# Gates z and n of a GRU step with the state as stationary operand, in four column groups

## The chip, the cores and the metric

The kernel runs on one core of a Trainium2 chip. The metric is the time of one execution in microseconds, as the device gives it. It is one program, written by hand for each engine: TensorE (PE), VectorE (DVE), ScalarE (ACT), GpSimd (POOL) and SyncE (SP) each have an instruction queue of their own, and semaphores join them.

## The reference

A GRU runs over 256 time steps of 16 sequences with 512 features, and its states go through a mixture of 8 experts of which each token uses the best two. The result is added to the input.

```python
def cell(h, x):
    gi = x @ W_ih + b_ih
    gh = h @ W_hh + b_hh
    i_r, i_z, i_n = jnp.split(gi, 3, axis=-1)
    h_r, h_z, h_n = jnp.split(gh, 3, axis=-1)
    r = jax.nn.sigmoid(i_r + h_r)
    z = jax.nn.sigmoid(i_z + h_z)
    n = jnp.tanh(i_n + r * h_n)
    h_new = (1.0 - z) * n + z * h
    return (h_new, h_new)
...
scores = jnp.einsum('btd,ed->bte', x, Wg)
topk_s, topk_i = jax.lax.top_k(scores, TOP_K)
probs = jax.nn.softmax(topk_s, axis=-1)
...
for e in range(E):
    h = jax.nn.silu(jnp.einsum('btd,hd->bth', x, W1[e])) * jnp.einsum('btd,hd->bth', x, W2[e])
    y = y + w[..., e:e + 1] * jnp.einsum('bth,dh->btd', h, W3[e])
...
x = x + _L0_ffn_ref(_L0_cond_ref(cond_2048, x, ...), ...)
```

All data are fp32. x is 16 x 256 x 512, W_ih and W_hh are 512 x 1536, the experts are 352 wide.

## The kernel before

Every fp32 matrix product is made of f16 products. A value is scaled and split into a high and a low f16 part (`whh[:, 0]` and `whh[:, 1]`, `hlog[..., 0/1, :]`), and three or four of the products of parts are summed in fp32 in PSUM. Features lie on the partitions: K = 4 blocks of P = 128 features, B = 16 columns for the sequences.

The recurrence is serial, T = 256 steps. One step on TensorE is `recur(t)`. The weights are the stationary operand (128 x 128) and the state is the moving one. First come 16 matmuls of the low weights of gate r with the high state (L1351, 16 columns), which wait for the semaphore value H_HI: VectorE's write of the high f16 part of the new state (L1080, first of two). Then, once the low part is there (H_LO, L1082), come 16 matmuls of r's high weights with both parts side by side (L1357, 32 columns). Then come 32 matmuls for n into `gn_ps` and 32 for z into `gz_ps` (L1366): 4 blocks of output, 4 of contraction, high and low weights behind each other, 32 moving columns each. Each of the three products counts `gh_ready` up by one.

PSUM is not cleared between steps. ScalarE seeds it for the next step (`seed`, L796): half the input projection of r or z, or half the bias of n, written to both halves, the matmuls add to it, and VectorE adds the two halves of the state (`halves`, L1054, a reduce over a pair).

The chain of a step on VectorE and ScalarE is `gru_step` and `gru_acts`: rpre (L1054), sigmoid (L810), hn (L1054), rh = r * hn (L1063), npre (L1067), tanh (L817), zpre (L1054), sigmoid of minus z (L819), nmh = n - h (L1073), znh (L1077), the new state as f16 (H_HI) and as fp32 (both L1080), and H_LO (L1082). `GRU` names these VectorE steps, and `gru(t, name)` is the value of the semaphore `gru_ops` at each. `behind_r(t)` and `behind_z(t)` put small work of the projection, the weight scaling and the routing between them.

All other work of TensorE is placed between two `recur` calls by a list, `blocks(t)`: input projections for four steps at a time (`project`, L1388, banks `gi_ps` and `b_ps`), for t from FIRST = 52 on an expert tile every four steps (A and B: the two up products, L1422; T and X: transposes; D0 and D1: the down product, L1458), and the routing of 128 tokens every eight steps (R1 and R2). 51 expert tiles run beside the recurrence and 20 behind it, in the tail. VectorE and ScalarE have their share of this work behind their part of each step; `choose(g)` (L1155 to L1176) is the routing part on VectorE. GpSimd's gathers and scatters, and SyncE's loads, wait for `gh_ready` to reach `behind_n(t)`.

## Time and profile before

| | us |
|---|---|
| time, median of 2 runs | 1504.82 |
| the two runs | 1501.98 and 1507.65 |
| span of the profiled execution, first to last instruction | 1501.1 |
| busy in it: TensorE / VectorE / ScalarE / GpSimd | 1409.4 / 1043.8 / 896.3 / 415.8 |
| chain that ended last | PE 83%, DVE 10%, issue 3% |

The profile is of one execution. It gives a span, and no other time of its own is recorded; the span lies 0.9 us under the lower of the two timed runs and 3.7 under their median. The busy time of an engine is what its instructions cover; on TensorE matmuls overlap, and their ends are modelled, so the distance between starts is the better measure of what one costs.

### The profile page before, as it was taken

How to read it: one execution, taken by the hardware profiler on the slowest of the kernel's cores; microseconds unless marked ns; L12 is line 12 of the kernel's file. 1: busy time of each engine (PE TensorE's matmuls, PEld its weight loads, DVE VectorE, ACT ScalarE, POOL GpSimd, SP SyncE). 2: the span in 40 equal slices, each digit the busy share in tenths (PEclk: the TensorE clock that was granted, in tenths of full speed). 3: DMA queues.
4: the chain of work that ended last, by engine and by line, in shares of the span. 5: the costliest groups of instructions: out<-in, count | busy, mean ns of one | idle time of the engine just before them, and what ended most of it. 6: DMA issues, size and time to landing. Idle time of an engine off the chain costs nothing.

```text
span 1501.1 us, 88729 instructions
## 1 busy us (share of the span) xinstructions
PE 1409.4 (94%) x37804; PEld 1227.2 (82%) x37804; DVE 1043.8 (70%) x4116; ACT 896.3 (60%) x2319; POOL 415.8 (28%) x850
## 2 busy tenths in 40 slices
PE   2888878899999999999999999999999999998997
PEld 1888778888888888888888888888888888885664
DVE  7788887777677677777777767776777776764333
ACT  6677675555565556655556555665556655555664
POOL 1011112123322232222332223222333222326443
PEclk9999887899999999999999999999999999999999
DMA  8445413112221222212222122211222212223431
GB/s 290 124 130 140 134 45 90 40 32 40 46 39 39 46 46 40 39 39 46 40 46 40 39 46 46 41 38 40 46 40 46 40 39 47 39 40 79 60 49 16
DMA packets 99011, 88.64 MB, mean 59 GB/s; under 512 B 41407, under 2 KB 74175, under 8 KB 98624
## 3 DMA queue, kind: packets, MB, share of 16 engines
q0 software_dynamic: 17952, 33.64, 12.9%
q1 hardware_dynamic: 80672, 49.32, 11.5%
q8 instruction: 306, 5.01, 1.5%
q14 instruction: 81, 0.66, 0.2%
HBM read 59.12 MB, written 35.72 MB: 63 GB/s over the span
## 4 chain that ended last, share of the span: by engine, by line
PE 83%; DVE 10%; issue 3%; ACT 1%; POOL 1%; DMA 1%; SPq 0%; DVEq 0%; POOLq 0%; ACTq 0%
PE gn_bank L1366 12%; PE gz_ps L1366 12%; PE y_ps L1458 9%; PE b_ps L1388 9%; PE a_ps L1422 8%; PE b_ps L1422 8%; PE gi_ps L1388 8%; PE gr_ps L1357 6%; PE gr_ps L1351 6%; DVE wexp L1037 2%; PE tr_ps L1436 2%; PE tr_ps L1446 2%; PE tr_ps L1478 1%; DVE npre L1067 1%; DVE nmh L1073 1%
## 5 line engine op out<-in xcount | busy, mean ns | idle before, releaser
L1366 PE MATMUL gz_ps<-hlog,whh 128*128 128x32 f16 x8192 | 246.0, 177 | 6.1 <-issue 6.0
L1366 PE MATMUL gn_bank<-hlog,whh 128*128 128x32 f16 x8192 | 245.2, 177 | 2.4 <-issue 2.2
L625 POOL DMA_INDIRECT out_y<-work,mt x57 | 93.9, 1648 | 546.2 <-PE gz_ps L1366 309.6
L1366 PEld LDWEIGHTS gz_ps<-hlog,whh 128*128 128x128 f16 x8192 | 224.1, 96 | 6.9 <-issue 6.7
L1366 PEld LDWEIGHTS gn_bank<-hlog,whh 128*128 128x128 f16 x8192 | 224.2, 96 | 2.7 <-issue 2.7
L1351 PEld LDWEIGHTS gr_ps<-hlog,whh 128*128 128x128 f16 x4096 | 130.6, 96 | 53.9 <-DVE hlog L1080 32.4
L1351 PE MATMUL gr_ps<-hlog,whh 128*128 128x16 f16 x4096 | 141.9, 170 | 31.3 <-DVE hlog L1080 28.3
L1388 PE MATMUL b_ps<-xs,wih 128*128 128x64 f16 x4752 | 162.3, 197 | 3.4 <-issue 2.1
L1458 PE MATMUL y_ps<-wexp,work 128*128 x639 | 159.0, 382 | 1.9 <-ACT work L845 1.9
L1388 PEld LDWEIGHTS b_ps<-xs,wih 128*128 128x128 f16 x4752 | 153.3, 101 | 5.1 <-issue 3.5
L810 ACT ACTIVATE rs<-rpre,sc 128x64 f32<-128x64 f32 x256 | 88.0, 344 | 112.7 <-DVE rpre L1054 112.5
L1388 PE MATMUL gi_ps<-xs,wih 128*128 128x64 f16 x4464 | 145.5, 194 | 4.7 <-issue 3.4
L1388 PEld LDWEIGHTS gi_ps<-xs,wih 128*128 128x128 f16 x4464 | 137.8, 99 | 6.7 <-issue 6.2
L1357 PE MATMUL gr_ps<-hlog,whh 128*128 128x32 f16 x4096 | 142.3, 177 | 1.0 <-issue 0.9
L636 POOL DMA_INDIRECT meta<-meta_sb,pos_i x64 | 66.0, 1031 | 242.4 <-PE gn_bank L1366 109.8
L1054 DVE TENSOR_REDUCE rpre<-gr_ps 128x64 f32<-128x128 f32 x256 | 73.8, 288 | 76.9 <-PE gr_ps L1357 74.5
L1357 PEld LDWEIGHTS gr_ps<-hlog,whh 128*128 128x128 f16 x4096 | 121.2, 96 | 1.3 <-issue 1.0
L1422 PE MATMUL a_ps<-wexp,xgt 128*128 x732 | 119.9, 313 | 0.2 <-issue 0.2
L1422 PE MATMUL b_ps<-wexp,xgt 128*128 x732 | 119.3, 313 | 0.0
L796 ACT ACTIVATE gn_bank<-bhn,sc 128x128 f32<-128x128 f32 x256 | 93.4, 365 | 40.0 <-DVE hn L1054 33.7
L839 ACT ACTIVATE hid<-work,hscale 128x352 f16<-128x352 f32 x71 | 41.8, 588 | 124.8 <-DVE hscale L1221 124.8
L1054 DVE TENSOR_REDUCE hn<-gn_bank 128x64 f32<-128x128 f32 x256 | 73.5, 287 | 51.3 <-PE gn_bank L1366 46.1
(217 smaller groups left out, 2550.3 us busy)
## 6 DMA issues: line engine op xcount, KB each, us to landing
wexp<-in_w_units SPq DMA_DIRECT2D x46, 256.0 KB, 3.8
x_raw<-in_x_feat SPq DMA_DIRECT2D x32, 256.0 KB, 3.7
out_y<-in_x_tok SPq DMA_DIRECT2D x16, 512.0 KB
h_tok<-xrow SPq DMA_DIRECT2D x32, 256.0 KB, 2.0
wexp<-in_w_hh SPq DMA_DIRECT2D x4, 768.0 KB, 6.8
wexp<-in_w_inproj SPq DMA_DIRECT2D x4, 768.0 KB, 11.8
wexp<-in_w_units SPq DMA_DIRECT2D x15, 192.0 KB, 4.5
mt<-meta SPq DMA_DIRECT2D x71, 1.0 KB, 1.7
```

The source lines that it names most:

```text
L625: pool.indirect_dma_start(out=out, out_offset=bass.IndirectOffsetOnAxis(ap=mt[:, j % RING, 0:1].bitcast(I32), axis=0), in_=ysc[y_slot(j)], ...
L636: pool.indirect_dma_start(out=meta, out_offset=bass.IndirectOffsetOnAxis(ap=pos_i[:, i:i + 1], axis=0), in_=meta_sb[:, g, i], in_offset=No ...
L796: S.activation(gh[:], values.unsqueeze(2).to_broadcast([P, K, 2, B]), ACT.Copy, scale=scale(SC_SEED)).then_inc(seeded, 1)
L810: S.activation(rs[:], rpre[:], ACT.Sigmoid, scale=scale(SC_INV)).then_inc(sig_r, 1)
L839: S.activation(hid16[:, 0, 0:HE], hid[:], ACT.Copy, scale=hscale[:, 0:1]).then_inc(hid_hi, 1)
L1054: op(V.tensor_reduce(dst, gh[:].rearrange("p k a b -> p k b a"), AX_X, ALU.add))
L1351: pe.matmul(gr_ps[:, j, 0], whh[:, 1, k, j * P:(j + 1) * P], h[:, k, 0], start=False, stop=False, skip_group_check=True)
L1357: mm = pe.matmul(gr_ps[:, j], whh[:, 0, k, j * P:(j + 1) * P], h[:, k], start=False, stop=True, skip_group_check=True)
L1366: mm = pe.matmul(dst[:, j], whh[:, i, k, m * P:(m + 1) * P], h[:, k], start=False, stop=True, skip_group_check=True)
L1388: mm = pe.matmul(BATCH_BANKS[bank][:, (m - first) * BTOK:(m - first + 1) * BTOK], wih[:, p, w_part, (b * K + k) * P:(b * K + k + 1) * P], ...
L1422: mm = pe.matmul(dst, xT[x_slot(j)][:, a * K + k], part[:, k], start=(i == 0 and k == 0), stop=(i == 2 and k == K - 1))
L1458: mm = pe.matmul(y_ps[:], hidT[:, PARTS[i][0] * HB + b], parts[PARTS[i][1]][:, b], start=((i, b) == DOWN[0]), stop=((i, b) == DOWN[-1]))
```

## The change

z and n are computed with the operands exchanged. The state of one block, 16 sequences with their high and low parts (32 columns, now laid out as pairs), is the stationary operand, and 256 columns of weights move: the 8 blocks of z and n, 32 features of each. The result of group g lies on the partitions 32g to 32g+31 of one bank, `zn_bank`, one partition for each sequence and part, one column for each feature. There are four groups, for each of the 4 blocks of contraction, high and low weights behind each other: 32 matmuls. The bank isn't seeded; the first matmul of each group clears it. z and n now share one count of `gh_ready`, two a step in place of three.

VectorE transposes n's half and z's half back in 32 x 32 blocks (`turn`) into the first two of three columns of `n_parts` and `z_parts`. The third holds n's bias (written once) and the input projection of z (`place_z`, ScalarE, each step). `total` sums the three. Gate r stays as it was. Some steps now write in place.

```diff
-    GRU = "R HN R_HN N_PRE Z N_H Z_NH H_HI H_NEW H_LO".split()
+    GRU = "R N_TURNED HN R_HN N_PRE Z_TURNED Z N_H Z_NH H_HI H_NEW H_LO".split()
...
-        return 3 * t + 2
+        return 2 * t + 2
...
-        hlog = sb("hlog", [P, 2, K, 2, P], F16)
+        hlog = sb("hlog", [P, 2, K, P, 2], F16)
...
+        n_parts = sb("n_parts", [P, K, B, 3])
+        z_parts = sb("z_parts", [P, K, B, 3])
...
-        gn_bank = ps("gn_bank", [P, 512])
-        gn_ps = gn_bank[:, 0:K * 2 * B].rearrange("p (k a b) -> p k a b", k=K, a=2)
-        gz_ps = ps("gz_ps", [P, K, 2, B])
+        zn_bank = ps("zn_bank", [P, 512])
+        z_ps, n_ps = (zn_bank[:, i * K * 2 * B:(i + 1) * K * 2 * B].rearrange("p (k b a) -> p k b a", k=K, a=2)
+                      for i in range(2))
...
-            def seed(gh, values, seeded):
-
-                S.activation(gh[:], values.unsqueeze(2).to_broadcast([P, K, 2, B]), ACT.Copy,
-                             scale=scale(SC_SEED)).then_inc(seeded, 1)
+            def seed_r(t):
+                S.activation(gr_ps[:], gi_of(t, 0).unsqueeze(2).to_broadcast([P, K, 2, B]), ACT.Copy,
+                             scale=scale(SC_SEED)).then_inc(r_seeded, 1)
+
+            def place_z(t):
+                S.activation(z_parts[:, :, :, 2], gi_of(t, 1), ACT.Copy, scale=scale(SC_PLACE)).then_inc(z_placed, 1)
...
-                S.activation(rs[:], rpre[:], ACT.Sigmoid, scale=scale(SC_INV)).then_inc(sig_r, 1)
+                S.activation(rpre[:], rpre[:], ACT.Sigmoid, scale=scale(SC_INV)).then_inc(sig_r, 1)
                 if t + 1 < T:
-                    seed(gr_ps, gi_of(t + 1, 0), r_seeded)
-                act.wait_ge(gru_ops, gru(t, "HN"))
-                if t + 1 < T:
-                    seed(gn_ps, bhn[:], n_seeded)
+                    seed_r(t + 1)
                 act.wait_ge(gru_ops, gru(t, "N_PRE"))
-                S.activation(nt[:], npre[:], ACT.Tanh).then_inc(tanh_n, 1)
+                S.activation(npre[:], npre[:], ACT.Tanh).then_inc(tanh_n, 1)
                 act.wait_ge(gru_ops, gru(t, "Z"))
-                S.activation(zs[:], zpre[:], ACT.Sigmoid, scale=scale(SC_MINUS)).then_inc(sig_z, 1)
+                S.activation(zpre[:], zpre[:], ACT.Sigmoid, scale=scale(SC_MINUS)).then_inc(sig_z, 1)
                 if t + 1 < T and not z_comes_late(t + 1):
-                    seed(gz_ps, gi_of(t + 1, 1), z_seeded)
+                    place_z(t + 1)
...
-                def halves(dst, gh):
-                    op(V.tensor_reduce(dst, gh[:].rearrange("p k a b -> p k b a"), AX_X, ALU.add))
-
-                dve.wait_ge(gh_ready, 3 * t + 1)
-                halves(rpre[:], gr_ps)
+                def total(dst, parts):
+                    op(V.tensor_reduce(dst, parts, AX_X, ALU.add))
+
+                def turn(parts, rows):
+
+                    op(V.transpose(parts[:, :, :, 0:2], rows))
+
+                dve.wait_ge(gh_ready, 2 * t + 1)
+                total(rpre[:], gr_ps[:].rearrange("p k a b -> p k b a"))
                 behind_r(t)
-                dve.wait_ge(gh_ready, 3 * t + 2)
-                halves(hn[:], gn_ps)
+                dve.wait_ge(gh_ready, 2 * t + 2)
+                turn(n_parts, n_ps)
+                after("N_TURNED")
+                total(hn[:], n_parts[:])
                 dve.wait_ge(sig_r, t + 1)
                 after("HN")
-                op(V.tensor_tensor(rh[:], rs[:], hn[:], ALU.mult))
+                op(V.tensor_tensor(hn[:], rpre[:], hn[:], ALU.mult))
                 after("R_HN")
                 if t % BS == 0:
                     dve.wait_ge(gi_taken, batches_upto(i, M))
-                op(V.scalar_tensor_tensor(out=npre[:], in0=rh[:], scalar=scale(SC_INV), in1=gi_n,
+                op(V.scalar_tensor_tensor(out=npre[:], in0=hn[:], scalar=scale(SC_INV), in1=gi_n,
                                           op0=ALU.mult, op1=ALU.add))
-                dve.wait_ge(gh_ready, 3 * t + 3)
-                halves(zpre[:], gz_ps)
+                turn(z_parts, z_ps)
+                dve.wait_ge(z_placed, t + 1)
+                after("Z_TURNED")
+                total(zpre[:], z_parts[:])
                 behind_z(t)
                 dve.wait_ge(tanh_n, t + 1)
-                op(V.scalar_tensor_tensor(out=nmh[:], in0=nt[:], scalar=scale(SC_H), in1=h_now[:, now],
+                op(V.scalar_tensor_tensor(out=nmh[:], in0=npre[:], scalar=scale(SC_H), in1=h_now[:, now],
                                           op0=ALU.mult, op1=ALU.subtract))
                 dve.wait_ge(sig_z, t + 1)
                 after("N_H")
-                op(V.tensor_tensor(znh[:], zs[:], nmh[:], ALU.mult))
+                op(V.tensor_tensor(nmh[:], zpre[:], nmh[:], ALU.mult))
                 after("Z_NH")
-                for dst in (parts[:, :, 0], h_now[:, new]):
-                    op(V.tensor_tensor(dst, h_now[:, now], znh[:], ALU.add))
+                for dst in (parts[:, :, :, 0], h_now[:, new]):
+                    op(V.tensor_tensor(dst, h_now[:, now], nmh[:], ALU.add))
                 after("H_NEW")
-                op(V.tensor_tensor(parts[:, :, 1], h_now[:, new], parts[:, :, 0], ALU.subtract))
+                op(V.tensor_tensor(parts[:, :, :, 1], h_now[:, new], parts[:, :, :, 0], ALU.subtract))
...
-                        pe.matmul(gr_ps[:, j, 0], whh[:, 1, k, j * P:(j + 1) * P], h[:, k, 0],
+                        pe.matmul(gr_ps[:, j, 0], whh[:, 1, k, j * P:(j + 1) * P], h[:, k, :, 0],
                                   start=False, stop=False, skip_group_check=True)
                 if t:
                     pe.wait_ge(gru_ops, gru(t - 1, "H_LO"))
                 for j in range(K):
                     for k in range(K):
-                        mm = pe.matmul(gr_ps[:, j], whh[:, 0, k, j * P:(j + 1) * P], h[:, k],
+                        mm = pe.matmul(gr_ps[:, j], whh[:, 0, k, j * P:(j + 1) * P], h[:, k].rearrange("p b a -> p a b"),
                                        start=False, stop=True, skip_group_check=True)
                 mm.then_inc(gh_ready, 1)
-                for dst, first, seeded in ((gn_ps, 2 * K, n_seeded), (gz_ps, K, z_seeded)):
-                    pe.wait_ge(seeded, t + 1)
-                    for j in range(K):
-                        m = first + j
-                        for k in range(K):
-                            for i in range(2):
-                                mm = pe.matmul(dst[:, j], whh[:, i, k, m * P:(m + 1) * P], h[:, k],
-                                               start=False, stop=True, skip_group_check=True)
-                    mm.then_inc(gh_ready, 1)
+
+                for k in range(K):
+                    for g in range(P // Q):
+                        for i in range(2):
+                            w = whh[:, i, k, K * P:M * P].rearrange("p (m x) -> p m x", x=P)
+                            mm = pe.matmul(zn_bank[g * Q:(g + 1) * Q, 0:4 * K * B], h[:, k].rearrange("p b a -> p (b a)"),
+                                           w[:, :, g * Q:(g + 1) * Q],
+                                           start=(k == 0 and i == 0), stop=(k == K - 1 and i == 1))
```

On TensorE, in one step of the main part of the recurrence (t from 52 on), the kernel before has this row:

```order
L1351 MATMUL gr_ps<-hlog,whh 128x16 x16
L1357 MATMUL gr_ps<-hlog,whh 128x32 x16
L1366 MATMUL gn_bank<-hlog,whh 128x32 x32
L1366 MATMUL gz_ps<-hlog,whh 128x32 x32
L1388 MATMUL gi_ps<-xs,wih 128x64 x72
L1458 ISA
L1458 MATMUL y_ps<-wexp,work 128x512 x4
L1351 MATMUL gr_ps<-hlog,whh 128x16 x16
```

and the changed kernel this one (ISA is the read of an expert's number into an address):

```order
L1357 MATMUL gr_ps<-hlog,whh 128x16 x16
L1363 MATMUL gr_ps<-hlog,whh 128x32 x16
L1371 MATMUL zn_bank<-whh,hlog 32x256 x32
L1394 MATMUL gi_ps<-xs,wih 128x64 x72
L1464 ISA
L1464 MATMUL y_ps<-wexp,work 128x512 x4
L1357 MATMUL gr_ps<-hlog,whh 128x16 x16
```

The two groups of 32 matmuls with 32 moving columns have become one group of 32 with 256 (32x256 is its result); what stands before and behind it has not moved.

On VectorE, in one early step, from the n total to the low part of the state, the kernel before has (etab is a table of the weight scaling):

```order
L1054 TENSOR_REDUCE hn<-gn_bank 128x64
L1063 TENSOR_TENSOR rh<-rs,hn 128x64
L1067 SCALAR_TENSOR_TENSOR npre<-rh,sc,gi 128x64
L1054 TENSOR_REDUCE zpre<-gz_ps 128x64
L1101 TENSOR_SCALAR etab<-prep_pw,sc 128x2
L1103 TENSOR_SCALAR etab<-prep_pw 128x2
L1073 SCALAR_TENSOR_TENSOR nmh<-nt,sc,h_now 128x64
L1077 TENSOR_TENSOR znh<-zs,nmh 128x64
L1080 TENSOR_TENSOR hlog<-h_now,znh 128x4x16
L1080 TENSOR_TENSOR h_now<-h_now,znh 128x64
L1082 TENSOR_TENSOR hlog<-h_now,hlog 128x4x16
```

and the changed kernel:

```order
L1054 STREAM_TRANSPOSE n_parts<-zn_bank 128x64x2
L1050 TENSOR_REDUCE hn<-n_parts 128x64
L1065 TENSOR_TENSOR hn<-rpre,hn 128x64
L1069 SCALAR_TENSOR_TENSOR npre<-hn,sc,gi 128x64
L1054 STREAM_TRANSPOSE z_parts<-zn_bank 128x64x2
L1050 TENSOR_REDUCE zpre<-z_parts 128x64
L1105 TENSOR_SCALAR etab<-prep_pw,sc 128x2
L1107 TENSOR_SCALAR etab<-prep_pw 128x2
L1077 SCALAR_TENSOR_TENSOR nmh<-npre,sc,h_now 128x64
L1081 TENSOR_TENSOR nmh<-zpre,nmh 128x64
L1084 TENSOR_TENSOR hlog<-h_now,nmh 128x4x16
L1084 TENSOR_TENSOR h_now<-h_now,nmh 128x64
L1086 TENSOR_TENSOR hlog<-h_now,hlog 128x4x16
```

Each of the two reduces has a transpose ahead of it, and reads what that wrote in place of the bank. The n reduce stood between the end of the n matmuls and that of the z matmuls; now both transposes stand behind the one group.

## Rows read from the trace of the kernel before

**Rows 1.** The page: busy time; granted TensorE clock in 40 equal slices, tenths.

```profile
PE 1409.4 (94%) x37804; PEld 1227.2 (82%) x37804; DVE 1043.8 (70%) x4116; ACT 896.3 (60%) x2319; POOL 415.8 (28%) x850
...
PEclk9999887899999999999999999999999999999999
```

**Rows 2.** Waits of TensorE (us in total, times, longest): 39:291, then 291:1348.

```profile
PE gr_ps L1351 <- DVE hlog L1080: 27.2, 29, 3.2
...
PE gi_ps L1388 <- issue: 3.4, 6, 0.7
...
PE gr_ps L1351 <- DVE hlog L1080: 0.5, 1, 0.5
```

**Rows 3.** Windows by stage: length, PE busy (x), clock; then of L1357 alone.

```profile
39.00:291.00 252.00, 209.29 (x6833) 0.87 0.35 102
291.00:1348.00 1057.00, 1051.16 (x29644) 1.00 0.21 41
...
39.00:291.00 252.00, 28.71 (x816) 24.41 (x816) 0.87 0.35 102
291.00:1348.00 1057.00, 112.45 (x3248) 95.86 (x3248) 1.00 0.21 41
```

**Rows 4.** Timeline of TensorE, 704 to 718 us (start, duration, line, x count).

```profile
704.51 2.26 PE L1388 MATMUL gi_ps<-xs,wih 128*128 128x64 f16 x72
...
708.12 0.55 PE L1351 MATMUL gr_ps<-hlog,whh 128*128 128x16 f16 x16
...
714.72 0.96 PE L1366 MATMUL gz_ps<-hlog,whh 128*128 128x32 f16 x32
...
717.68 0.55 PE L1351 MATMUL gr_ps<-hlog,whh 128*128 128x16 f16 x16
```

**Rows 5.** Timeline of all engines, one early step, 65 to 68 us.

```profile
65.59 0.95 PE L1366 MATMUL gz_ps<-hlog,whh 128*128 128x32 f16 x32
65.78 0.29 DVE L1054 TENSOR_REDUCE hn<-gn_bank 128x64 f32<-128x128 f32 x1 [0.19 <-PE gn_bank L1366]
...
66.18 0.23 DVE L1063 TENSOR_TENSOR rh<-rs,hn 128x64 f32<-128x64 f32 x1
...
66.44 0.28 DVE L1067 SCALAR_TENSOR_TENSOR npre<-rh,sc,gi 128x64 f32<-128x64 f32 x1
66.64 0.28 DVE L1054 TENSOR_REDUCE zpre<-gz_ps 128x64 f32<-128x128 f32 x1
...
66.96 0.35 ACT L819 ACTIVATE zs<-zpre,sc 128x64 f32<-128x64 f32 x1
...
67.44 0.23 DVE L1077 TENSOR_TENSOR znh<-zs,nmh 128x64 f32<-128x64 f32 x1
...
67.70 0.22 DVE L1080 TENSOR_TENSOR hlog<-h_now,znh 128x64 f16<-128x64 f32 x1
...
67.98 0.56 PE L1351 MATMUL gr_ps<-hlog,whh 128*128 128x16 f16 x16 [0.38 <-DVE hlog L1080]
```

**Rows 6.** Timeline of TensorE, wider matmuls; then their group, with the mean of one.

```profile
715.55 1.96 PE L1422 MATMUL a_ps<-wexp,xgt 128*128 x12
...
1493.13 2.11 PE L1458 MATMUL y_ps<-wexp,work 128*128 x9 [0.97 <-ACT work L845]
...
L1458 PE MATMUL y_ps<-wexp,work 128*128 x639 | 159.0, 382 | 1.9 <-ACT work L845 1.9
...
L1422 PE MATMUL a_ps<-wexp,xgt 128*128 x732 | 119.9, 313 | 0.2 <-issue 0.2
```

**Rows 7.** Groups by line: busy us, mean ns of one, idle before.

```profile
L1366 PE MATMUL gz_ps<-hlog,whh 128*128 128x32 f16 x8192 | 246.0, 177 | 6.1 <-issue 6.0
...
L1054 DVE TENSOR_REDUCE hn<-gn_bank 128x64 f32<-128x128 f32 x256 | 73.5, 287 | 51.3 <-PE gn_bank L1366 46.1
```

**Rows 8.** Timeline of VectorE, 706.8 to 709.9 us.

```profile
706.81 0.62 DVE L1019 SCALAR_TENSOR_TENSOR gi<-gi_ps,gi_inv,gi_bias 128x384 f32<-128x384 f32 x1 [0.17 <-PE gi_ps L1388]
...
709.82 0.28 DVE L1054 TENSOR_REDUCE rpre<-gr_ps 128x64 f32<-128x128 f32 x1
```

More of the change, by code:

```diff
@@ L54, in gru_moe_kernel @@
     assert GS == 8 and E == 8 and HE == 352 and TILES == 71 and FULL == 57
+    Q = 2 * B
+    assert Q == 32 and P // Q == K
     FIRST = 52
@@ L903, in _ @@
             act.wait_ge(gates_open, 1)
-            seed(gr_ps, gi_of(0, 0), r_seeded)
-            seed(gn_ps, bhn[:], n_seeded)
-            seed(gz_ps, gi_of(0, 1), z_seeded)
+            seed_r(0)
+            place_z(0)
             for t in range(T):
@@ L933, in _ @@
                 if t + 1 < T and z_comes_late(t + 1):
-                    seed(gz_ps, gi_of(t + 1, 1), z_seeded)
+                    place_z(t + 1)
             take_rows(LAST)
@@ L1253, in _ @@
             x_largest(0)
-            chain(V.tensor_copy(bhn[:], bias[:, 1, 2 * K:M].unsqueeze(2).to_broadcast([P, K, B])))
             x_scale(0)
@@ L1265, in _ @@
             first = h_parts(2 * GS - 1)
-            chain(V.tensor_copy(first[:, :, 0], h_now[:, 0]))
-            chain(V.tensor_tensor(first[:, :, 1], h_now[:, 0], first[:, :, 0], ALU.subtract))
+            chain(V.tensor_copy(first[:, :, :, 0], h_now[:, 0]))
+            chain(V.tensor_tensor(first[:, :, :, 1], h_now[:, 0], first[:, :, :, 0], ALU.subtract))
             chain(V.tensor_scalar(scale(SC_GAP), scale(SC_PG), 2.0 ** -14, scale(SC_IH), ALU.mult, ALU.mult))
@@ L1296, in _ @@
             chain(V.tensor_scalar(scale(SC_MINUS), scale(SC_INV), -1.0, None, ALU.mult))
+            chain(V.tensor_scalar(scale(SC_PLACE), scale(SC_W), scale(SC_H), None, ALU.mult))
+            chain(V.tensor_scalar(n_parts[:, :, :, 2], bias[:, 1, 2 * K:M].unsqueeze(2).to_broadcast([P, K, B]),
+                                  scale(SC_PLACE), None, ALU.mult))
             assert n_setup[0] == N_SETUP, n_setup
@@ L1477, in turn_rows @@
                         at = (i * K + k) * P
-                        mm = pe.transpose(tr_ps[:, at:at + P], h[:, k, i], ident[:])
+                        mm = pe.transpose(tr_ps[:, at:at + P], h[:, k, :, i], ident[:])
                 mm.then_inc(tr_mm, 1)
@@ L1481, in turn_rows @@
                     for k in range(K):
-                        mm = pe.matmul(route_ps(g)[:, 0:2 * E], h[:, k, i],
+                        mm = pe.matmul(route_ps(g)[:, 0:2 * E], h[:, k, :, i],
                                        wg[:, k].rearrange("p e h -> p (e h)"),
@@ L1545, in _ @@
             pe.wait_ge(setup, N_CONSTS)
-            for gh in (gr_ps, gn_ps, gz_ps):
-                mm = pe.matmul(gh[:].rearrange("p k a b -> p (k a b)"), ident[:], ident[:], start=True, stop=True)
-            mm.then_inc(gates_open, 1)
+            pe.matmul(gr_ps[:].rearrange("p k a b -> p (k a b)"), ident[:], ident[:], start=True, stop=True
+                      ).then_inc(gates_open, 1)
             turn_x_exponent(0)
```

22 lines of the change are left out of this document (8 added, 14 removed).

## Prediction

> **What bounds the kernel now.** I read the page first: PE is busy in 94% of the span, and the granted clock is full except in slices 6 to 10 [rows 1]. The waits say the same from the other side: TensorE sat idle for the new state (the f16 write of H_HI) for 27.2 us in the first 51 steps, and for 0.5 us in the 203 behind them [rows 2]. The windows cut the span into three stages, and the count of the r gate's matmuls (16 a step) gives the steps of each [rows 3]: early, 252 us for 816/16 = 51 steps, 4.94 us each, PE at 83% and mean clock 0.87; main, 1057 us for 3248/16 = 203 steps, 5.21 us each, PE at 99%, clock 1.00; the tail, 153 us, holds the last two steps and the last expert tiles.
>
> Then the timeline of TensorE over four main steps (the longest and the shortest stand in [rows 4]). A step starts with the low r matmul and holds r low 0.40, r high 0.40, n 0.80, z 0.80 us (from start to start), 2.40 in all, then the projection and expert work, which I call the cover. It runs from its own start, 0.80 behind that of z, to the next r start: 708.12-704.51 = 3.61 and 717.68-(714.72+0.80) = 2.16; the one between reads 2.60, the one behind 2.87; mean 2.81. The mean step less 2.40 gives 2.81 too. While TensorE works on the cover, VectorE and ScalarE finish the step. So the main stage asks whether the chain of the gates is shorter than the cover.
>
> That chain is best read where nothing else stands in it: an early step [rows 5]. The z matmuls start at 65.59, the last of 32 at 66.37 (first start to last end 0.95 us, 177 ns for one [rows 7]: (0.95-0.18)/31 = 25 ns apart). The next r matmul starts at 67.98, 1.61 us later, and 0.28 behind the start of H_HI. 1.61 is under every cover of rows 4. TensorE binds the main stage, and the chain has 0.5 to 2.0 us of slack there.
>
> **The change, TensorE.** 64 matmuls of 32 moving columns (25 ns each, 1.60 us a step) become 32 of 256 moving columns, each on 32 columns of the array. No row shows 256 columns or a column group. The nearest are 12 matmuls of 352 columns in 1.96 us, (1.96-0.31)/11 = 150 ns apart, and 9 of 512 columns in the tail's y groups, (2.11-0.38)/8 = 216 ns apart [rows 6]: 0.42 to 0.43 ns a column, so 109 ns for 256. How many of the four groups stream at once decides:
> - one at a time: 32 x 109 = 3.49 us;
> - all four: 8 x 109 = 0.87 us;
> - two: 16 x 109 = 1.74 us.
> I take two. In every row here matmuls start in the order of the program, and if that holds across groups, the low weights of group 0 must wait for their own columns until the high ones have streamed, and group 1 stands behind them. Only the low matmul of one group and the high one of the next then overlap, 16 pairs. The Trainium skill has this as a rule (TensorE: Matmul & The Clock Gate, "Part 3: Packing small matmuls — row/col tiling"): matmuls of different tiles overlap with starts some 4 ns apart, yet matmuls start and end strictly in program order. No run here shows either half; by its first half alone one would plan with 0.87, by both with 1.74. Changing between whole array and groups twice a step is in no row: from 0 (matmuls follow each other 25 ns apart here whatever bank they write) to 0.2 us, 0.18 being the whole of one small matmul from its start to its end [rows 7]; I take 0.
>
> **The change, the chain.** All of z and n now comes at one point, so what VectorE did for n beside the z matmuls moves behind the last matmul, and two transposes join it. Counted from the last matmul's start, with the starts of rows 5: first transpose at +0.31 (hn stood 0.22 behind the last n start, plus 0.09 for 224 more columns at 0.43 ns); n total at +0.64; rh at +1.06 (hn to rh was 0.40, and 64 more elements are read); npre +1.32 (0.26); second transpose +1.52 (0.20, as npre to zpre); z total +1.92 (two waits, as hn to rh); sigmoid of z +2.26 (0.32, plus the longer read); znh +2.74 (0.48); H_HI +3.00 (0.26); next r matmul +3.28 (0.28). Tanh and nmh lie beside the z total. No row shows a transpose: below, 0.23 of a 64-element operation [rows 5], above, 0.62 of one on 384 elements from PSUM [rows 8]; I take 0.29, that of the reduce of the same 128 PSUM elements [rows 7]. The ends move the chain by -0.12 or +0.66. The Trainium skill (VectorE: DVE Perf Modes, "The three transpose paths") gives 311 ns for a 128x128 bf16 block transpose; with it the chain would be 0.04 longer.
>
> ScalarE loses the n seed and writes half as much for z; these stand behind the sigmoids and were off the path, so I count nothing. The strided state, the setup's smaller start and the point at which the queues of POOL and SP go on (2t+2 is now the end of z and n, where it was the end of n, 0.94 us later: 1.74 against 0.80) count nothing: no wait of TensorE in main is for a transfer, and the largest of its waits there is 3.4 us in total [rows 2].
>
> **The sum, main.** Step = 0.80 (r) + group time + the larger of cover and 3.28. Of four covers 3.61 alone exceeds 3.28: mean 3.36. With 1.74: 5.90. Once in eight steps VectorE also has a 3.0 us block behind H_LO (706.81 to 709.82, with 0.2 of waiting [rows 8]), until now hidden by a cover of 3.61. H_LO ends at +3.63, this block at +6.6, the r reduce at +6.9, where the groups were ready at 3.28+0.80+1.74+0.31 = 6.1: 0.8 us, 0.10 a step. 6.00-5.21 = 0.79, by 203 = +160 us.
> Early, where the chain is open already: chain +1.67, groups +0.14, together 1.81. The step there is 4.94 where 2.40+1.61 = 4.01 would do; of these 0.93 us of other waits I let a third vanish under the longer chain: +1.5, by 51 = +77 us.
> Clock: in main PE falls from 99% to (0.80+1.74+2.81)/6.00 = 89%, midway to the early stage with 0.87. Half clock in 8% of the time, each such step 3 us longer (r, groups and part of the cover at half speed): 0.24 x 203 = +49. Bounds 0 and twice that.
> The span is 1501.1; 1501.1+160+77+49 = 1787. The two timed runs are 1501.98 and 1507.65, their median 3.7 above the span, so 1791; I say 1790.
>
> **Rivals.**
> - *Four wide.* Each group takes a second matmul in waiting, and order does not matter: 0.87. For it: starts 25 ns apart show instructions are handed over far faster than 109 ns. Step 0.80+0.87+3.36, plus 0.21 for the eighth step = 5.24: +6 in main; early (1.67-0.73-0.2) x 51 = +38; clock +49: 1501+93+4 = 1598. Slower even so: the chain has become the bound.
> - *One at a time.* Step 0.80+3.49+3.36 = 7.65: +495; early 3.26 x 51 = +166; clock +20: 2186. Then the change does not do what it says. Nothing here excludes it: every row uses the whole array.
> - *Not slower.* Four wide, transposes at 0.23, so a chain of 3.16, and the clock full. The mean of the larger is 3.27, the step 4.94, or 5.15 with the VectorE block: main -55 to -12; early (1.54-0.73-0.2) x 51 = +31: 1481 to 1524, and below 1475 if two or three links overlap more than counted. It decides below a chain of about 3.2 us; against it stands that every link is a measured one.
>
> **Chances.** Two wide 0.40 (1700 to 1920), four wide 0.32 (1530 to 1680), one at a time 0.13, not slower 0.15. About 2% is what a measurement of this kernel can tell from no change: faster 0.07, same 0.08, slower 0.85. The range reaches down over four wide and up over the clock and a 0.62 us transpose: 1530 to 1920.
>
> **What would show it.** The 32 group matmuls' start-to-start over a step (1.7, 0.9 or 3.5 us); the r matmul's wait for H_HI in nearly every main step, about 0.5 us or more; last group matmul to next r matmul near 3.28; transposes near 0.29; the granted clock in main. I am wrong if main steps keep 5.2 us, or if that wait stays absent.

## The result and the profile after

| | before | changed |
|---|---|---|
| time, median of 2 runs, us | 1504.82 | 1571.60 |
| the two runs | 1501.98, 1507.65 | 1570.74, 1572.46 |
| span of the profiled execution | 1501.1 | 1569.0 |

The ratio is 1.0432 (95% interval 1.0405 to 1.0459): slower by 4.3%, where I had said slower by 19%. The direction and the new bound were right, the size was not.

The page of the changed kernel: busy time by engine, TensorE's busy tenths and granted clock in 40 slices, and the shares of the chain that ended last. It answers to [rows 1].

```profile
PE 1342.6 (86%) x29610; PEld 1046.7 (67%) x29610; DVE 1205.9 (77%) x4629; ACT 818.1 (52%) x2063; POOL 411.3 (26%) x850
...
PE   2767676779999999999999999999999999987997
...
PEclk9787877879999999999999999999999999998999
...
DVE 46%; PE 37%; ACT 8%; issue 7%; POOL 1%; DMA 1%; DVEq 1%; SPq 0%; another core or an unknown queue 0%; ACTq 0%; POOLq 0%
```

TensorE does 67 us less than before and yet the kernel ends 68 us later. The chain that ended last was 83% PE; now VectorE has the largest share. The same is to be seen in TensorE's waits, here of the main stage (where the step's first r matmul waits for H_HI); [rows 2] had 0.5 us for it:

```profile
PE gr_ps L1357 <- DVE hlog L1084: 80.8, 129, 1.2
```

The three stages in the windows (length, then busy time and count of PE, PEld, DVE, ACT and POOL, granted clock, DMA share, GB/s), and r's high matmuls, 16 a step, that give the steps; they answer to [rows 3]:

```profile
39.80:335.50 295.70, 211.12 (x5200) 178.22 (x5201) 238.03 (x897) 151.54 (x357) 35.80 (x106) 0.77 0.28 85
335.50:1406.70 1071.20, 978.40 (x23148) 772.66 (x23145) 876.14 (x3471) 555.05 (x1517) 298.79 (x626) 1.00 0.19 40
1406.70:1569.00 162.30, 141.79 (x1105) 88.79 (x1105) 60.05 (x187) 85.58 (x157) 70.87 (x99) 0.94 0.28 48
```
```profile
39.80:335.50 295.70, 28.91 (x816) 0.77 0.28 85
335.50:1406.70 1071.20, 112.48 (x3248) 1.00 0.19 40
```

With [rows 3] this splits the 67.9 us: the early 51 steps went from 4.94 to 5.80 us (+44), the main 203 from 5.21 to 5.28 (+14), the tail from 153.0 to 162.3 (+9), the start gave +0.6. So two thirds of the loss are early, where only 51 steps are, and the main stage is nearly as it was although every step in it changed.

How a main step looks now: TensorE's timeline (start, length, line, operation, count, idle before):

```profile
767.55 0.56 PE L1357 MATMUL gr_ps<-hlog,whh 128*128 128x16 f16 x16 [0.87 <-DVE hlog L1084]
767.96 0.55 PE L1363 MATMUL gr_ps<-hlog,whh 128*128 128x32 f16 x16
768.45 1.07 PE L1371 MATMUL zn_bank<-whh,hlog 128*32 128x256 f16 x32
769.45 1.96 PE L1428 MATMUL b_ps<-wexp,xgt 128*128 x12
771.25 1.24 PE L1464 MATMUL y_ps<-wexp,work 128*128 x5
772.67 0.38 PE L1357 MATMUL gr_ps<-hlog,whh 128*128 128x16 f16 x9 [0.18 <-DVE hlog L1084]
```

and VectorE's of the same step, from n's transpose to H_HI:

```profile
769.58 0.32 DVE L1054 STREAM_TRANSPOSE n_parts<-zn_bank 128x128 f32<-128x128 f32 x1 [0.19 <-PE zn_bank L1371]
769.93 0.35 DVE L1050 TENSOR_REDUCE hn<-n_parts 128x64 f32<-128x192 f32 x1
770.39 0.23 DVE L1065 TENSOR_TENSOR hn<-rpre,hn 128x64 f32<-128x64 f32 x1
770.65 0.28 DVE L1069 SCALAR_TENSOR_TENSOR npre<-hn,sc,gi 128x64 f32<-128x64 f32 x1
770.85 0.31 DVE L1054 STREAM_TRANSPOSE z_parts<-zn_bank 128x128 f32<-128x128 f32 x1
771.26 0.35 DVE L1050 TENSOR_REDUCE zpre<-z_parts 128x64 f32<-128x192 f32 x1
771.53 0.28 DVE L1077 SCALAR_TENSOR_TENSOR nmh<-npre,sc,h_now 128x64 f32<-128x64 f32 x1
772.03 0.31 DVE L1081 TENSOR_TENSOR nmh<-zpre,nmh 128x64 f32<-128x64 f32 x1 [0.22 <-ACT zpre L816]
772.38 0.23 DVE L1084 TENSOR_TENSOR hlog<-h_now,nmh 128x64 f16<-128x64 f32 x1
```

From the first r matmul to the last group matmul a main step takes 1.69 us (median of the starts), where r, n and z took 2.38: the 32 group matmuls need 0.79 us from first to last start, and the first of them starts 0.11 behind r's last, where matmuls on the whole array follow each other by 0.025. From the last group matmul to the next r matmul the open chain (a step in which TensorE waits for it) takes 3.34 us, where it took 1.61 in the step of [rows 5]. So TensorE gave up 0.7 us ahead of the chain, and the chain grew by 1.7; in most steps it is now longer than the cover.

The groups that carry it (count | busy, mean ns | idle before); they answer to [rows 7]:

```profile
L1371 PE MATMUL zn_bank<-whh,hlog 128*32 128x256 f16 x8192 | 295.9, 288 | 0.3 <-issue 0.3
```
```profile
L1050 DVE TENSOR_REDUCE zpre<-z_parts 128x64 f32<-128x192 f32 x256 | 90.4, 353 | 26.9 <-DVE z_parts L1054 0.5
L1054 DVE STREAM_TRANSPOSE n_parts<-zn_bank 128x128 f32<-128x128 f32 x256 | 80.9, 316 | 54.2 <-PE zn_bank L1371 44.5 <-remote 3.1
L1054 DVE STREAM_TRANSPOSE z_parts<-zn_bank 128x128 f32<-128x128 f32 x256 | 79.4, 310 | 0.0
```

A group matmul lasts 288 ns by the profile, whose ends are modelled, yet 32 of them start within 0.79 us. That is 109 ns for four: four groups wide.

The main steps repeat with a period of eight. A step is 1.69 us and then the longer of the cover and the chain. The values are medians; the cover is read here from the start of the last group matmul to the start of the last matmul ahead of the next r matmul:

| t mod 8 | 0 | 1 | 2 | 3 | 4 | 5 | 6 | 7 |
|---|---|---|---|---|---|---|---|---|
| step before, us | 4.78 | 5.47 | 6.02 | 4.99 | 4.54 | 5.27 | 5.36 | 4.97 |
| step after | 5.04 | 5.04 | 5.69 | 5.63 | 5.04 | 5.12 | 5.11 | 5.57 |
| cover after | 2.77 | 3.02 | 3.97 | 2.76 | 2.45 | 2.87 | 2.96 | 2.71 |

Only step 2 is still bound by its cover. Steps 0, 1 and 4 show the bare chain; 5 and 6 add up to 0.1. Step 3 carries VectorE's routing block: it ends late enough that n's transpose begins at 759.33, 0.96 us behind the last group matmul in place of 0.34, so 0.6 us late. Step 7 is held by ScalarE, whose queue has three wide operations ahead of r's sigmoid (ScalarE, then VectorE, of that step):

```profile
779.11 0.59 ACT L836 ACTIVATE hid<-work,hscale 128x352 f16<-128x352 f32 x1 [1.65 <-DVE hscale L1225]
779.60 0.67 ACT L867 ACTIVATE work<-y_ps,yscale 128x512 f32<-128x512 f32 x1
780.17 0.62 ACT L734 ACTIVATE xrow<-x_raw 128x512 f16<-128x512 f32 x1
...
780.78 0.34 ACT L810 ACTIVATE rpre<-rpre,sc 128x64 f32<-128x64 f32 x1
```
```profile
781.15 0.23 DVE L1065 TENSOR_TENSOR hn<-rpre,hn 128x64 f32<-128x64 f32 x1 [0.64 <-ACT rpre L810]
```

The long steps of before (1, 2, 5 and 6) got shorter and the short ones longer; that is how +0.07 comes out of two changes of some 0.7 us and more.

### The profile page after: what moved, and what is told of

It is laid out like the page before. It is cut to its first block, busy times and chain, and to the rows that moved or that the text cites. A ratio compares the mean times of both kernels' runs of the same rounds, so it can differ in the third digit from the quotient of the medians.

```text
span 1569.0 us, 72852 instructions
## 1 busy us (share of the span) xinstructions
PE 1342.6 (86%) x29610; PEld 1046.7 (67%) x29610; DVE 1205.9 (77%) x4629; ACT 818.1 (52%) x2063; POOL 411.3 (26%) x850
## 4 chain that ended last, share of the span: by engine, by line
DVE 46%; PE 37%; ACT 8%; issue 7%; POOL 1%; DMA 1%; DVEq 1%; SPq 0%; another core or an unknown queue 0%; ACTq 0%; POOLq 0%
PE zn_bank L1371 13%; PE gr_ps L1357 6%; DVE zpre L1050 5%; PE gr_ps L1363 5%; DVE hn L1050 5%; ACT zpre L816 5%; PE b_ps L1428 5%; DVE npre L1069 4%; DVE n_parts L1054 4%; PE y_ps L1464 4%; DVE nmh L1081 4%; DVE hlog L1084 3%; DVE z_parts L1054 3%; DVE hn L1065 3%; DVE gi L1015 2%
## 5 line engine op out<-in xcount | busy, mean ns | idle before, releaser
L1371 PE MATMUL zn_bank<-whh,hlog 128*32 128x256 f16 x8192 | 295.9, 288 | 0.3 <-issue 0.3
L1357 PE MATMUL gr_ps<-hlog,whh 128*128 128x16 f16 x4096 | 143.6, 170 | 157.8 <-DVE hlog L1084 155.8
L1357 PEld LDWEIGHTS gr_ps<-hlog,whh 128*128 128x128 f16 x4096 | 120.4, 96 | 217.9 <-DVE hlog L1084 216.3
L1371 PEld LDWEIGHTS zn_bank<-whh,hlog 128*32 128x32 f16 x8192 | 211.6, 101 | 15.3 <-issue 0.9
L814 ACT ACTIVATE npre<-npre 128x64 f32<-128x64 f32 x256 | 65.8, 257 | 293.0 <-DVE npre L1069 291.3
L816 ACT ACTIVATE zpre<-zpre,sc 128x64 f32<-128x64 f32 x256 | 89.1, 348 | 109.7 <-DVE zpre L1050 108.8
L810 ACT ACTIVATE rpre<-rpre,sc 128x64 f32<-128x64 f32 x256 | 88.8, 347 | 98.3 <-DVE rpre L1050 97.6
L1054 DVE STREAM_TRANSPOSE n_parts<-zn_bank 128x128 f32<-128x128 f32 x256 | 80.9, 316 | 54.2 <-PE zn_bank L1371 44.5
L1363 PEld LDWEIGHTS gr_ps<-hlog,whh 128*128 128x128 f16 x4096 | 120.9, 96 | 0.0
L1050 DVE TENSOR_REDUCE zpre<-z_parts 128x64 f32<-128x192 f32 x256 | 90.4, 353 | 26.9 <-DVE z_parts L1054 0.5
L612 POOL DMA_INDIRECT xgt<-h_tok,mt x52 | 55.8, 1073 | 208.0 <-PE zn_bank L1371 200.8
L797 ACT ACTIVATE z_parts<-gi,sc 128x64 f32<-128x64 f32 x256 | 94.4, 369 | 19.0 <-DVE gi L1015 18.9
```

The source lines that it names most:

```text
L797: S.activation(z_parts[:, :, :, 2], gi_of(t, 1), ACT.Copy, scale=scale(SC_PLACE)).then_inc(z_placed, 1)
L810: S.activation(rpre[:], rpre[:], ACT.Sigmoid, scale=scale(SC_INV)).then_inc(sig_r, 1)
L816: S.activation(zpre[:], zpre[:], ACT.Sigmoid, scale=scale(SC_MINUS)).then_inc(sig_z, 1)
L1050: op(V.tensor_reduce(dst, parts, AX_X, ALU.add))
L1054: op(V.transpose(parts[:, :, :, 0:2], rows))
L1357: pe.matmul(gr_ps[:, j, 0], whh[:, 1, k, j * P:(j + 1) * P], h[:, k, :, 0], start=False, stop=False, skip_group_check=True)
```

## Experiments

Two questions. How do the column groups share the array, which decides the term that I had wrong? And what in the chain costs most, and can it be had for less? Each ratio is to the kernel before as timed beside the run: its medians there were 1507.03 us (order of the groups, group by group, n first then z, z ahead of n), 1511.29 (four in a row, the joining point, both) and 1508.36 (the turn alone).

**Order of the groups.** The 32 matmuls with the groups in turn, low and high of one no longer behind each other:

```diff
-                    for g in range(P // Q):
-                        for i in range(2):
+                    for i in range(2):
+                        for g in range(P // Q):
```

> The changed kernel, but the high weights of all four groups come first and then the low weights (loops k, part, group in place of k, group, part): no group has two matmuls directly behind each other. Theory A (each group takes a second matmul in waiting, so all four stream at once whatever the order): the 32 matmuls keep 109 ns for four, 0.79 us from first to last start, and the time stays within 0.5% of the changed kernel's 1571.6 us. Theory B (program order holds a group back behind the one ahead, and the 0.79 us of the changed kernel are already the worse order): the same 32 matmuls get shorter, and the time falls by up to 1% where they stand on the path.

Measured: 1565.71 us, ratio to before 1.0400 (1.0378 to 1.0423); groups 0.784 us, main step 5.26, chain 3.33. Against the changed kernel's 1571.60 that is 0.4% less, and the two intervals overlap: that low and high stand in pairs costs nothing that matters. In the changed kernel the 32 starts are 7, 7, 7 and 89 ns apart, over and over; here 3, 3, 4 and 99. So in both four matmuls start together every 109 ns. The records don't name a matmul's group, but two of one group start 109 ns apart (the next run), so these four are one of each. Then in the changed kernel the high one of group 3 starts ahead of the low one of group 0, which stands before it in the program.

**Group by group.** All eight matmuls of a group, then the next group:

```diff
-                for k in range(K):
-                    for g in range(P // Q):
+                for g in range(P // Q):
+                    for k in range(K):
                         for i in range(2):
```

> The changed kernel with the groups one after the other, eight matmuls of one group in a row (loops group, k, part). Theory A with room for one matmul in waiting: group 1 can start only when six of group 0's eight have streamed, so the last start comes at about 3 x 6 x 109 + 7 x 109 ns = 2.7 us in place of 0.79. As the chain of the gates is the bound, the whole 1.9 us go onto each of 256 steps: 1571 + 490 = 2060 us, chain from last group matmul to next r matmul still about 3.35 us. Theory C (the queue ahead of the groups is deep, 8 or more): 0.8 to 0.9 us as before, 1572 us.

Measured: 1858.17 us, ratio 1.2346 (1.2321 to 1.2371); groups 2.135 us, main step 6.43, early 6.87, chain 3.31. Eight in a row do matter, though by less than the 2060 us that I expected. The windows count the group matmuls begun from the first start to later times, first of the changed kernel, then of this one (columns: window, length, busy (count), clock, DMA share, GB/s):

```profile
763.21:763.27 0.06, 0.05 (x4) 1.00 0.00 0
...
763.21:763.60 0.39, 0.38 (x16) 1.00 0.00 0
```
```profile
763.66:763.72 0.06, 0.05 (x1) 1.00 0.99 171
763.66:763.83 0.17, 0.16 (x2) 1.00 1.19 205
...
763.66:764.05 0.39, 0.38 (x4) 1.00 1.09 194
...
763.66:764.26 0.60, 0.59 (x8) 1.00 1.10 198
```

Sixteen in 0.39 us there, four at a time; here one, two and, in 0.39 us, four, one every 109 ns, and then two at a time. The second group begins as the fifth matmul of the first starts (some 0.45 us in), when 6, 7 and 8 are still to come. That fits a group with one matmul streaming and three waiting, and a queue behind it that goes on to the next group once its eighth is taken up. My forecast of 2.7 us had a single one in waiting.

**Four in a row** tests that number: with one streaming and three waiting, four of one group block nobody.

```diff
-                for k in range(K):
+                for k2 in range(0, K, 2):
                     for g in range(P // Q):
-                        for i in range(2):
+                        for k, i in itertools.product((k2, k2 + 1), range(2)):
```

> The changed kernel with four matmuls of one group behind each other (two blocks of contraction, high and low), then four of the next group, twice over. In the run with eight in a row the next group began 454 ns in, when the fifth matmul of the group ahead began, so three seem to wait for a group beside the one that streams. Theory A (a queue of its own for each group, one streaming and three waiting): four in a row still fit, all groups start within 0.05 us of each other, first to last start 0.8 us, time within 0.5% of the changed kernel. Theory D (one window over all groups, of four or so matmuls past the oldest that has not started): only two groups overlap, first to last start 1.7 us or more, 200 us more in all. Theory B (strict program order) would give 2.7 us and 2050 us.

Measured: 1578.94 us, ratio 1.0453 (1.0426 to 1.0479); groups 0.819 us, main step 5.32. Starts are 14, 13, 13 and 66 to 80 ns apart: all four groups run at once, which rules out theory D (1.7 us or more). From one group's first matmul to the next group's it is 3.4 ns where one matmul of each group stands in a row, 7 with two, 13 to 14 with four: each hand-over takes about 3.4 ns, and little else is lost (0.819 against 0.79 us).

**The joining point alone.** The kernel before, where n's sum waits until z is there too:

```diff
-                dve.wait_ge(gh_ready, 3 * t + 2)
+                dve.wait_ge(gh_ready, 3 * t + 3)
                 halves(hn[:], gn_ps)
```

> The kernel before, with one thing of the change alone: VectorE's sum of n waits until z is complete too, as if both came at one point. Chain from the last z matmul to the next r matmul, from the rows: 2.4 us in place of 1.6. Theory 'the main stage has slack, the early stage has none': main covers are 2.2 to 3.6 us, so main steps grow by at most 0.1 us (20 us in all), early ones by up to 0.8 us (20 to 40 us): 1530 to 1560 us. Rival 'joining the two points costs nothing and the transposes are all of it': 1507 us.

Measured: 1535.15 us, ratio 1.0160 (1.0134 to 1.0186); chain 2.41 us, main step 5.27 (+0.06, or 12 us), early 5.24 (+0.30, or 15 us). A chain that is 0.8 us longer costs 24 us by the medians (the profiled executions differ by 35, of which 8 are in the tail): the main stage has slack for most of it, as the prediction said, the early stage has not. Of the 1.73 us by which the changed kernel's chain is longer, 0.8 is thus the joining point. The two transposes are most of the rest: from their starts to those of the sums behind them it is 0.35 and 0.41 us in the step shown above, 0.76 together. That part is an estimate, since no run has the transposes without the joining point.

**n first, then z.** Two banks and two halves of 128 columns, so that n's work on VectorE lies beside z's matmuls again:

```diff
-                for k in range(K):
-                    for g in range(P // Q):
-                        for i in range(2):
-                            w = whh[:, i, k, K * P:M * P].rearrange(...)
-                            mm = pe.matmul(zn_bank[g * Q:(g + 1) * Q, 0:4 * K * B], ...)
-                mm.then_inc(gh_ready, 1)
+                for bank, m in ((zn_bank, 2 * K), (z_bank, K)):
+                    for k in range(K):
+                        for g in range(P // Q):
+                            for i in range(2):
+                                w = whh[:, i, k, m * P:(m + K) * P].rearrange(...)
+                                mm = pe.matmul(bank[g * Q:(g + 1) * Q, 0:2 * K * B], ...)
+                    mm.then_inc(gh_ready, 1)
```

> The changed kernel with n and z apart again: 32 matmuls of 128 columns for n, then 32 for z into a bank of its own, each with its own count, so that n's transpose, sum and the rest start while z is computed. Theory 'the chain behind the last matmul is the bound' : the chain from the last z matmul to the next r matmul shortens from 3.35 us by as much as n is early. If the small matmuls stream four wide at 128 columns (0.44 us for each half) it is about 2.95 us, main steps 4.9 us in place of 5.28, the whole 1480 to 1500 us. If a floor of 25 ns for each matmul holds (the weight loads were 25 ns apart), n and z take 0.80 us each, chain 2.6 us, main steps 5.3 to 5.45 us, the whole 1570 to 1600 us. Rival theory 'VectorE is simply too busy': no gain in either case, since its instructions are the same.

Measured: 1524.77 us, ratio 1.0129 (1.0109 to 1.0150), 47 us less than the changed kernel, with VectorE's instructions unchanged. The chain came out (2.97 us open), and 64 matmuls of 128 columns took 0.868 us from first to last start, 0.07 more than 32 of 256. The whole did not reach the forecast, since I had summed the bare chain for all main steps: measured 5.14 us, as step 3 (5.61) and step 7 (5.38) keep their VectorE block and ScalarE queue, and step 2 (5.72) its cover. TensorE also stands idle here for reasons other than the chain, of which more below.

**z's chain ahead of n's.** Both transposes, both sums, then n's product; ScalarE takes z's sigmoid ahead of the tanh:

```diff
                 turn(n_parts, n_ps)
                 after("N_TURNED")
+                turn(z_parts, z_ps)
                 total(hn[:], n_parts[:])
+                dve.wait_ge(z_placed, t + 1)
+                after("Z_TURNED")
+                total(zpre[:], z_parts[:])
...
                 op(V.scalar_tensor_tensor(out=npre[:], ...))
-                turn(z_parts, z_ps)
-                dve.wait_ge(z_placed, t + 1)
-                after("Z_TURNED")
-                total(zpre[:], z_parts[:])
```

> The changed kernel with VectorE's order altered: both transposes first, then n total, z total, then r times n and npre; ScalarE does the sigmoid of z ahead of tanh. No instruction is added or left out. Theory 'the serial chain is the bound': it now ends in tanh, nmh, znh; counted from the rows, 3.1 us in place of 3.35, so about 0.2 us off each main step and each early one: 1571 - 50 = 1520 us. Rival 'VectorE's total work is the bound': same time within 0.5%.

Measured: 1491.54 us, ratio 0.9904 (0.9884 to 0.9924); chain 3.06, main step 5.00. Same operations, other order, 80 us less than the changed kernel, where I expected 50: the chain is 0.28 shorter, not 0.2, and steps 3 and 7 lose about 0.5 each. The rival, that VectorE's total work is the bound, is out, since that work is the same. This step starts n's transpose at 766.33 and writes H_HI 2.44 us later; the step above took 2.80:

```profile
766.33 0.32 DVE L1054 STREAM_TRANSPOSE n_parts<-zn_bank 128x128 f32<-128x128 f32 x1 [0.22 <-PE zn_bank L1371]
766.58 0.28 DVE L1054 STREAM_TRANSPOSE z_parts<-zn_bank 128x128 f32<-128x128 f32 x1
766.77 0.31 DVE L1050 TENSOR_REDUCE hn<-n_parts 128x64 f32<-128x192 f32 x1
767.00 0.34 DVE L1050 TENSOR_REDUCE zpre<-z_parts 128x64 f32<-128x192 f32 x1
767.26 0.21 DVE L1069 TENSOR_TENSOR hn<-rpre,hn 128x64 f32<-128x64 f32 x1
...
768.77 0.23 DVE L1084 TENSOR_TENSOR hlog<-h_now,nmh 128x64 f16<-128x64 f32 x1
```

The five starts are 0.25, 0.19, 0.23 and 0.26 apart. In the changed kernel's step an operation that needs the result just ahead of it starts 0.35 or 0.41 (transpose to sum) and 0.46 (sum to product) behind it. It isn't so everywhere: the product's result is needed at once too, and `npre` starts 0.26 behind it.

**Both, and the turn alone.** n first, with z's transpose put between n's sum and the product; and the changed kernel with only this one line moved (and its place in `GRU`, the list of semaphore values):

```diff
                 total(hn[:], n_parts[:])
+                turn(z_parts, z_ps)
                 dve.wait_ge(sig_r, t + 1)
...
                 op(V.scalar_tensor_tensor(out=npre[:], ...))
-                turn(z_parts, z_ps)
```

> n and z apart as in the earlier run of that kind (32 matmuls of 128 columns each), and z's transpose put ahead of r times n on VectorE, so that z's total ends some 0.4 us earlier. Theory 'the serial chain is the bound': last z matmul to next r matmul 2.5 to 2.6 us in place of 2.97 (apart) and 3.06 (z before n), below most covers; main steps 4.7 to 4.8 us, the whole 1430 to 1460 us, faster than the kernel before by 3 to 5%. Rival 'VectorE's work is the bound, reordering only moves the wait': 1490 us or more.

> The changed kernel with z's transpose put between n's total and r times n on VectorE, and nothing else moved: 32 matmuls of 256 columns, z and n at one point. In the run with z before n the chain still ended in tanh and nmh (3.06 us from the last group matmul to the next r matmul). Theory 'the serial chain is the bound': from its rows n's total starts 0.2 us sooner, npre at +1.4, z's total at +1.6, sigmoid at +2.0, next r matmul at 2.95 to 3.0; covers of 2.5 to 4.0 us then bind two or three of eight steps. Main steps 4.95 us, the whole 1480 to 1490 us, 1 to 2% faster than before. TensorE has the 61 instructions a step fewer that the run with n and z apart lacked, so its idle time for nothing the profile shows (40 us there in the main stage) should be under 15 us. Rival: same as the run with z before n, 1492, or slower, since the two transposes back to back were what gained there.

Measured, for both: 1487.60 us (1476.66 to 1488.56), ratio 0.9827 (0.9780 to 0.9874), chain 2.57, main step 5.02, early 5.23. Measured, the turn alone: 1475.59 us, ratio 0.9773 (0.9746 to 0.9800), chain 2.96, main step 4.92, early 5.30. One moved line takes 96 us off the changed kernel and gives the lowest median of all, 2.3% under the kernel before and a little below the 1480 to 1490 that I expected. Of the 101 us between the two profiled executions, 72 are in the main stage (0.35 a step, for a chain 0.38 shorter), 26 in the early one and 4 in the tail. Its VectorE, in a main step:

```profile
769.89 0.32 DVE L1054 STREAM_TRANSPOSE n_parts<-zn_bank 128x128 f32<-128x128 f32 x1
770.24 0.35 DVE L1050 TENSOR_REDUCE hn<-n_parts 128x64 f32<-128x192 f32 x1
770.51 0.31 DVE L1054 STREAM_TRANSPOSE z_parts<-zn_bank 128x128 f32<-128x128 f32 x1
770.74 0.18 DVE L1066 TENSOR_TENSOR hn<-rpre,hn 128x64 f32<-128x64 f32 x1
770.96 0.28 DVE L1070 SCALAR_TENSOR_TENSOR npre<-hn,sc,gi 128x64 f32<-128x64 f32 x1
771.16 0.34 DVE L1050 TENSOR_REDUCE zpre<-z_parts 128x64 f32<-128x192 f32 x1
...
772.22 0.23 DVE L1084 TENSOR_TENSOR hlog<-h_now,nmh 128x64 f16<-128x64 f32 x1
```

n's sum to product is 0.50 with the whole transpose in between, where it was 0.46 without it; the product to npre to z's sum then follows without the transpose and its 0.41. The wait for H_HI in main fell to 22.8 us, from 80.8:

```profile
PE gr_ps L1357 <- DVE hlog L1084: 22.8, 74, 0.9
```

The kernel with both has the shorter chain and is still not faster in main, against my forecast of 4.7 to 4.8. Its own waits in main:

```profile
PE gi_ps L1397 <- issue: 17.2, 23, 1.9
PE b_ps L1397 <- issue: 8.4, 16, 0.9
PE z_bank L1374 <- issue: 5.4, 10, 1.0
PE gr_ps L1359 <- DVE hlog L1086: 4.1, 10, 0.8
```

The columns are total, times and longest. H_HI holds it for 4.1 us only, but at three lines alone TensorE stands idle for 31 us ("issue") for nothing that the profile's waits show, up to 1.9 us at a time; n first, then z, shows 11.3 and 6.8 us of it at the same two lines. Without 39 us of such idle time in all, the 203 main steps would average 4.83 us, close to the forecast. Both runs have 8192 matmuls more than the changed kernel, but their number alone isn't it: the kernel before has as many (37804), and its largest such wait in the main stage is 3.4 us in total.

The trace points at the supply of instructions. The DMA queue that the page calls `instruction` (q8) moves 306 packets of 16 KB in this run and in the kernel before, 242 in the changed kernel. In the main stage of this run 34 idle stretches of this kind are longer than 0.4 us, 28 us together, and each of them ends 1.1 to 1.55 us behind the landing of such a packet; of all moments of the stage, about 11% lie at such a distance. In n first, then z, it is 21 of 21 (1.1 to 1.6 us), in the kernel before 6 of 6 (1.3 to 1.65); the changed kernel has none so long. So TensorE seems to run out of instructions where many short matmuls start 14 ns apart. No run tests it, so the cause stays open.

The same run shows without inference that starts leave the program's order. All of n's matmuls (`zn_bank`) stand ahead of all of z's (`z_bank`) in the program; at this place, behind a short halt, one of n's starts behind three of z's:

```profile
755.06 0.24 PE L1374 MATMUL z_bank<-whh,hlog 128*32 128x128 f16 x3
755.11 0.22 PE L1374 MATMUL zn_bank<-whh,hlog 128*32 128x128 f16 x1
```

## Why the prediction was right in direction and wrong in size

- **"I take two" failed.** This is the step that carried the forecast. Groups cost 0.79 us and not 1.74; r's first to the last group matmul is 1.69 where I had 2.54. The reason I gave was that "matmuls start in the order of the program, and if that holds across groups". It doesn't hold: all runs fit a group with one matmul streaming and three waiting, so that up to four in a row cost next to nothing (0.79 us for two, 0.82 for four, 2.14 for eight in a row). The rule that I set beside it (the Trainium skill, TensorE: Matmul & The Clock Gate, "Part 3: Packing small matmuls — row/col tiling"), that starts are strictly in program order, is contradicted by the starts of the changed kernel, of four and of eight in a row, and by the lines with `z_bank` ahead of `zn_bank` (with the groups in turn both orders are the same); its other half, starts some 4 ns apart, agrees with 3.4 ns here. The evidence for four wide stood in my own text, that instructions are handed over far faster than 109 ns, and I gave it 0.32. No row of before could settle it; what I could have done is to see that the rows only showed order on the *whole* array, where matmuls of different groups don't exist.
- **The switch between whole array and groups**, which I took at 0, costs nearly the 0.2 us that I had as its upper bound, half of it each way: the first group matmul starts 0.11 us behind r's last, 0.08 more than the usual 0.025, and the first matmul of the cover starts, in most steps, 205 ns behind the last group matmul, of which 109 are the time of that matmul's own 256 columns. (Behind one of 128 columns, some 56 ns, it is 152.) The way back lies in the cover, where an open chain hides it.
- **The clock term in main (+49) was 0.** TensorE is busy in 978.4 of 1071.2 us, 91%, and the granted clock is 1.00, as before. I had drawn a line between two stages, at 99% and 83% busy; the clock did not follow it. Its size was off as well: a mean clock midway between 1.00 and 0.87 is half clock in 13% of the time, not 8%. Early the clock did fall, from 0.87 to 0.77. Over the kernel the time at half clock went from 72 to 153 us, none of it in the main stage. (The clock of before is below 0.9 in slices 5 to 8 of [rows 1], not 6 to 10.)
- **The chain was right**: 3.28 forecast, 3.34 measured, and in the wait for H_HI, as the text said it would show. Transposes took 316 and 310 ns (0.29 forecast), the sums of 192 elements 353 (the reduce of before took 287), r's H_HI to its matmul 0.29 (0.28). The figure of 311 ns (the Trainium skill, VectorE: DVE Perf Modes, "The three transpose paths") for bf16 agrees with these fp32 ones.
- **The logic "larger of cover and chain" was right**, and the rival that used it with 0.87 forecast a main step of 5.24: measured 5.28. That it came so close is partly luck, as two sizes in it were off in opposite ways: the routing block costs 0.6 us in one step of eight (0.8 forecast for two wide, 1.67 for four), and the ScalarE queue ahead of r's sigmoid, which nothing of mine held, 0.5 in another.
- **The signs of being wrong.** One was that main steps keep 5.2 us, and at 5.28 they nearly do: the direction came out right because of the early stage, not because of the main stage, where I had put 209 of the 286 us, the clock's 49 among them. The other, that the wait for H_HI stays absent, didn't come: it stands in 129 of 203 main steps, 0.63 us on average, where I had said nearly every one. So the new bound is shown, and its price in the main stage was far too high.
- **Early**: +77 forecast, +38 by the four-wide rival, +44 measured, with the clock's fall in it.
- **The tail** I left at nothing; it is 9 us longer. The last two steps are longer, TensorE waits 2.08 and 4.26 us there (before: 0.56 and 1.53), and the granted clock of the first 33 us is 0.85, where it was 1.00. How much of it is the change is open: in the joining point alone, with the work of the kernel before, the tail is also 8 us longer.

The four terms give the miss: main (6.00-5.28) x 203 = 146, clock 49, early 33, less 9 for the tail, 219 of the 218 us between 1790 and 1571.6 (the sum rounds). Nearly all of it is the first bullet (it holds for main and early) and the clock.

Why the change lost is shown in the main. The joining point alone costs the kernel before 24 us, the order of the groups nothing as long as all four run, and one place in the order of the chain's operations 96 us, more than the whole loss of 67. TensorE's part of the change is a gain: its 0.69 us stand ahead of the chain, so they come off every step, open chain or not. Group by group shows it from the other side, where 1.34 us more of group time make a main step 1.15 longer. The loss is that the chain grew by more than this, 1.7 us, and covers of 2.5 to 3.0 us no longer hide it. How much of the early stage's +44 us is the lower clock and how much the chain no run separates.

## What to carry to other kernels

Before counting on faster matmuls in a recurrence, compare the chain of the other engines with the cover that is left behind the matmuls: here 0.7 us came off every step on TensorE, 1.7 went on the chain, and the chain is now the longer of the two in most steps. Where two results arrive at one point, try an order of the vector operations in which those with the longest spacing stand behind one they don't depend on; that order was worth 6% in this kernel, and it is one line. For matmuls on separate column groups, one, two or four of a group in a row made no difference of note here, and eight cost 18% over the changed kernel.

## What I had not expected of the hardware

- Four column groups stream side by side, 109 ns for four matmuls of 256 columns, and the runs with two, four and eight in a row fit one matmul running and three waiting in each; a hand-over takes about 3.4 ns. Across groups, starts are not in the program's order.
- 64 matmuls of 128 columns in groups start within 0.868 us, 14 ns apart, below the 25 ns that small matmuls on the whole array keep from each other in the kernel before.
- Going from the whole array to the groups costs 0.08 us, and going back 0.10.
- On VectorE a sum of 192 elements and the product that needs it start 0.46 us apart, and the same product behind an independent transpose starts 0.23 behind that.
- TensorE can stand idle up to 1.9 us in the kernel with n and z apart, and its longer halts end 1.1 to 1.55 us behind a landing on the `instruction` queue.
